# Attention on one core: the vector engine's order within a unit, and softmax sums by a reduction

## The reference, cut to what matters

```
q = ln(fp8_linear(x, wq))       # per head of 128, 16 heads
k = ln(fp8_linear(x, wk))       # 8 key heads; cross: from the context
v = fp8_linear(x, wv)
p = softmax(q k^T / sqrt(128))  # 64 x 64 for each head and batch element
o = p v
cat  = [o_self, o_cross]
catq = fp8(bf16(clip(cat / smooth, -448, 448)))
x = x + catq wproj * scale
```

## Time and profile before

| | us |
|---|---|
| median of three runs | 1179.42 |
| lowest, highest | 1179.37, 1182.78 |
| the profiled execution | 1184.29 |
| its span, first to last instruction | 1182.6 |
| TensorE busy (matmul) | 897.4 |
| VectorE busy | 909.8 |
| ScalarE busy | 727.6 |
| GpSimd busy | 391.3 |

### The profile page before, as it was taken

How to read it: one execution, slowest core, us unless ns; L and a number is a source line. 1 busy time by engine, 2 the same in 40 slices (tenths; PEclk the granted TensorE clock), 3 DMA queues, 4 the chain that set the end, 5 groups by cost and what they waited for, 6 DMA issues and landing times. The chain is left out here.

```text
span 1182.6 us, 23732 instructions
## 1 busy us (share of the span) xinstructions
PE 897.4 (76%) x6878; PEld 793.9 (67%) x6878; DVE 909.8 (77%) x2442; ACT 727.6 (62%) x2471; POOL 391.3 (33%) x498
## 2 busy tenths in 40 slices
PE   3720066423999999999998469999999999997638
PEld 2610033213888888888888458888888888887627
DVE  7989989887888888888888447777777777776471
ACT  3454044374878878877887357777777777774313
POOL 0009900000334444444443443343333433333124
PEclk9865589756999999999999569999999999998559
DMA  6022100002000000000000120000000000000400
GB/s 217 1 108 71 36 1 0 0 0 107 2 2 0 0 0 0 0 0 0 0 0 1 46 79 6 6 6 9 4 4 4 9 4 4 0 0 1 147 19 18
DMA packets 18265, 26.95 MB, mean 23 GB/s; under 512 B 1264, under 2 KB 15408, under 8 KB 17456
## 3 DMA queue, kind: packets, MB, share of 16 engines
q1 hardware_dynamic: 17840, 25.41, 6.3%
q0 software_dynamic: 384, 1.05, 0.3%
HBM read 23.83 MB, written 2.62 MB: 22 GB/s over the span
## 5 line engine op out<-in xcount | busy, mean ns | idle before, releaser
L1213 POOL TENSOR_TENSOR c_cat<-c_tb,c_mb 128x512 fp32r<-128x512 bf16 x64 | 74.3, 1161 | 143.8 <-DVE c_tb L1291 143.8
L1213 POOL TENSOR_TENSOR s_cat<-s_tb,s_mb 128x512 fp32r<-128x512 bf16 x64 | 74.1, 1158 | 112.8 <-DVE s_tb L1291 112.8
L1386 ACT ACTIVATE c_p<-c_kT_sc_ps,c_nmax 128x64 f32<-128x64 f32 x256 | 76.7, 312 | 53.5 <-DVE c_nmax L1257 53.5
L1403 PE MATMUL s_qo_ps<-wq,s_xqf 128*128 128x512 f32 x256 | 76.0, 419 | 32.5 <-POOL s_xqf L1195 32.5
L1386 ACT ACTIVATE s_p<-s_kT_sc_ps,s_nmax 128x64 f32<-128x64 f32 x256 | 76.7, 312 | 26.8 <-DVE s_nmax L1257 23.8
L1403 PE MATMUL c_qo_ps<-wq,c_xqf 128*128 128x512 f32 x256 | 77.0, 423 | 17.2 <-DVE wv L645 17.1
L1461 PE MATMUL s_pj_ps<-wp,s_cat 128*128 128x256 f32 x512 | 79.6, 300 | 1.5 <-POOL s_cat L1213 1.5
L1461 PE MATMUL c_pj_ps<-wp,c_cat 128*128 128x256 f32 x512 | 79.0, 298 | 1.5 <-POOL c_cat L1213 1.5
L1218 POOL TENSOR_TENSOR c_pn<-c_p,c_rsum 128x256 f32<-128x256 f32 x64 | 39.2, 613 | 115.0 <-DVE c_rsum L1340 115.0
L1218 POOL TENSOR_TENSOR s_pn<-s_p,s_rsum 128x256 f32<-128x256 f32 x64 | 39.2, 613 | 112.0 <-DVE s_rsum L1340 112.0
L1333 DVE TENSOR_TENSOR c_yb<-c_qo_ps,c_ism 128x512 bf16<-128x512 f32 x64 | 44.3, 692 | 37.8 <-PE c_qo_ps L1438 37.8
(11 more groups left out here) (359 smaller groups left out, 2899.4 us busy)
## 6 DMA issues: line engine op xcount, KB each, us to landing
x_res<-in_x SPq DMA_DIRECT2D x4, 512.0 KB, 6.0
vT<-in_ctxT SPq DMA_DIRECT2D x2, 1024.0 KB, 10.8
tf_work<-in_wqT SPq DMA_DIRECT2D x2, 1024.0 KB, 5.9
tf_work<-in_wprojT SPq DMA_DIRECT2D x2, 1024.0 KB, 5.5
w_work<-in_wqxT SPq DMA_DIRECT2D x2, 1024.0 KB, 6.5
w_work<-in_wkvxT SPq DMA_DIRECT2D x2, 1024.0 KB, 8.2
c_ctx<-in_ctxT SPq DMA_DIRECT2D x16, 128.0 KB, 2.2
w_work<-in_wprojT SPq DMA_DIRECT2D x2, 1024.0 KB, 7.3
```

The costliest lines, as they stand in the source:

```text
L1213: nc.gpsimd.tensor_tensor(cat[out8.o % 2][:], tb[:], mb[:], ALU.subtract).then_inc(cat_ready, 1)
L1386: nc.scalar.activation(pe_s[:, a * S:(a + 1) * S], sc_ps[:, a * S:(a + 1) * S], ACT.Exp, bias=nmax[:, a:a + 1], accum_out=psum_s[:, a:a + ...
L1403: last = nc.tensor.matmul(out_ap, x_col(h), w_pair[part][:, h, c0:c1], start=(n == 0), stop=(n == 2 * KC - 1))
```

## The change

On VectorE's step: all four rounding steps now come first, one after the other, right behind the scaling; then the residual addition (and statistics); then the three Newton steps, and `qn` right behind them; then the maxima; then `kn`. `qn` waits only for the transposes of the query of the unit before, `kn` for those of the key. The exponentials on ScalarE have no accumulator any more; a reduction on VectorE sums the four blocks of `p` (128x256 to 128x4) in front of the reciprocal, which waits for it by a new semaphore.

```diff
@@ VectorE, in step @@
-                    def normalised():
+                    def normalised_query():
                         dve.wait_ge(r_ready, u.count(1, 1))
-                        wait_unit(dve, t_done, u.before(1))
+                        wait_unit(dve, tq_done, u.before(1))
                         nc.vector.tensor_tensor(qn[:].rearrange("p (h d) -> p h d", d=D),
...
+
+                    def normalised_key():
                         dve.wait_ge(v_ready, u.count(1, 1))
+                        wait_unit(dve, t_done, u.before(1))
                         nc.vector.tensor_tensor(kn[:].rearrange("p (h d) -> p h d", d=D),
...
                     if u.live:
                         norm_guess()
-                    for part in range(3):
-                        if f8.live:
+                    if f8.live:
+                        for part in range(4):
                             round8(part)
-                        if u.live:
-                            newton(part)
                     if pj.live and pj.o % UT == UT - 1:
...
-                    if f8.live:
-                        round8(3)
+                    if u.live:
+                        for part in range(3):
+                            newton(part)
+                        normalised_query()
                     if sm.live:
                         maxima()
                     if u.live:
-                        normalised()
+                        normalised_key()
...
                     if sm.live:
                         dve.wait_ge(exp_ready, sm.count(4, 4))
                         wait_unit(dve, pn_ready, sm.before(1))
+                        nc.vector.tensor_reduce(psum_s[:], pe_s[:].rearrange("p (a t) -> p a t", a=4), AX.X, ALU.add
+                                                ).then_inc(sum_ready, 1)
+                        dve.wait_ge(sum_ready, sm.count(1, 1))
                         nc.vector.reciprocal(rsum[:], psum_s[:]).then_inc(rsum_ready, 1)
@@ ScalarE, in step @@
                             nc.scalar.activation(pe_s[:, a * S:(a + 1) * S], sc_ps[:, a * S:(a + 1) * S], ACT.Exp,
-                                                 bias=nmax[:, a:a + 1], accum_out=psum_s[:, a:a + 1]
-                                                 ).then_inc(exp_ready, 1)
+                                                 bias=nmax[:, a:a + 1]).then_inc(exp_ready, 1)
```

More of the change, by code:

```diff
@@ L1143, in attention_stage @@
         sc_done, max_ready, exp_ready = sg("sc_done"), sg("max_ready"), sg("exp_ready")
+        sum_ready = sg("sum_ready")
         rsum_ready, pn_ready = sg("rsum_ready"), sg("pn_ready")
```

## The result

The changed kernel takes 1311.9 us (median of four runs, 1308.1 to 1313.7) against 1180.3 us; the ratio is 1.111, 95% interval 1.107 to 1.114. The profiled execution has a span of 1311.6 us, 129 us over the 1182.6 us of the trace that the earlier trace rows come from. The forecast was +111 us, 1290.4 us, with a range up to 1320.

The account below looks back on a forecast made before the run. The vector engine's loop was taken to bind, by 0.2 us over TensorE. First stage 67 us plus second stage 46 us, less 2 us, gave +111 us, 1290.4 us, with a range of 1263 to 1320.

Parts of the forecast that it names:

- The hold by `cat`: VectorE's second Newton step is held until GpSimd's `cat` ends: 0.91 us in each of 61 units a stage.
- The bound with a second step free under `cat`: Second Newton step not held, third held instead: `qn` 1.72 us after `tb`, 0.20 us less a unit, 24 us in all.
- The sum: New VectorE reduction of the exponentials in front of the reciprocal: 0.40 us, and 0.04 for the wait behind it.
- `yb` to the sum of squares 0.69: VectorE loop term: 0.69 us between these starts, with the reciprocal.
- the 1.04 us to the clip: VectorE loop term: 1.04 us from the start of the sum of squares to the clip.
- The units that carry more: Units with casts, GpSimd additions, residual addition or statistics pay extra: means 6.88 and 6.81 us against the ordinary 6.58.
- rival 3: TensorE, less busy, is at times granted its lower clock, 1.2 GHz: 71 us more, 1361 us; chance 0.06.
- The upper end: 1320 us, if `cat` is prolonged by 0.08 us (10 us) and the exponentials come late (20 us).
- Exponentials at nothing: ScalarE, outside the loop, saves the accumulator reads: gains nothing, but lets exponentials end at +2.00 us, before the sum at +2.11.
- The upper bound for slow ones, 20 us: Exponentials on ScalarE still 0.30 us apart would end at +2.27 us, costing the loop 0.16 us, 20 us in all.
- Rival 1: `cat` doesn't hold the Newton steps: +15 us in the first stage, +3 in the second, 1197 us; chance 0.09.
- The rival "faster": Sum costs nearly nothing, Newton runs free, TensorE's 5.43 us a unit decides: at most 33 us gained, 1146 us; chance 0.03.

Follow-up runs that it names:

- the kernel without it: Changed kernel with one more wait on GpSimd, so the subtraction into `cat` starts only after the unit's third Newton step: 1207.5 us.
- other orders: Kernels with accumulators, no sum, residual addition and statistics behind `kn`, and `tb` and maxima behind `qn` in either order: 1168.1 and 1168.7 us against the kernel before's 1180.1 to 1180.7.

## Why the prediction was right, and what it undersized

- **The hold by `cat`.** No row of the kernel before had this pair; it was carried over from other pairs, and it is shown now by the trace and by two experiments that change the start or the length of `cat`. `tb` to `qn` was put at 1.92, with the second step held, and at 2.12 behind the residual addition; it is so in 65 and 30 units. In 24 units, those with the index 0 and 1 of a round, the second step slips in front of `cat` and the third is held instead, with `qn` at +1.80; the forecast did not have that. The margin is small: the second step starts 0.54 us after `tb` (put at 0.61), `cat` 0.50, but 0.59 in these 24. The hold is worth about 104 us: the kernel without it is at 1207.5. The bound with a second step free under `cat` is out: whenever it starts there it is held. Nor did `cat` get longer (1.16 us).
- **The Trainium skill's rule** ("SBUF — State Buffer", section "SBUF: two separate sides"), an exclusive lock for the whole instruction: with `cat` at 1.16 us the step takes 1.15, with 0.43 it takes 0.42. The trace agrees in all 122 cases. Not everything on VectorE is held, though: in the kernel before, 61 `qn` a stage start under `cat` and keep their 0.68 us; in the changed kernel the statistics (at 872.30 in the trace, under a `cat` from 871.83 on), which read SBUF, keep their 0.43 us in all 15 cases. In the changed kernel itself no maxima and no `kn` lie beside GpSimd work, so there they say nothing.
- **The sum** was put at 0.40 plus 0.04 and takes 0.41 plus 0.03. But the reduction's cost in the loop was undersized: the sum of squares also starts 0.08 us later behind the reciprocal, which the term "`yb` to the sum of squares 0.69" left out, and takes 0.95 us instead of 0.92, which the 1.04 us to the clip left out: 0.11 us a unit. And the turn of the loop, 0.39 us in one unit of eight, was in no term. Together 0.11 + 0.05 = 0.16 us.
- **The units that carry more** were a little oversized: the second rounding step ends 0.08 us late, not 0.13 (0.37 instead of 0.29), since it starts 1.39 after the sum of squares and GpSimd's addition ends at 1.61, and the scaling with the cast is held 0.50, not 0.60. That gives back some 0.06 us in the first stage. In the second, units with casts take 0.58 us more than ordinary ones (7.28 against 6.70), where 0.73 was forecast: 0.04 us in the mean.
- **The sum of all.** Steady intervals are 6.99 and 6.93 us, forecast 6.88 and 6.81: 0.11 and 0.12 too little, 61 times each, 14 us of the 18 that the spans differ from the forecast. Of the rest, some 2 us lie in the first intervals of the two stages and 2 us outside of them.
- **The clock (rival 3).** In the first stage the granted clock is 0.97 in the mean from 300 to 720 us, where it was 1.00 (300 to 650 us): with TensorE busy 339 of 420 us it falls to the lower of its two levels, 1.2 GHz, eight times for a short while. So rival 3 came true in a small part: five intervals of the steady first stage are 0.2 to 0.5 us longer than those at the same place in other rounds, about 1.5 us together. In the second stage it stays at 1.00 (780 to 1200 us), with TensorE busy 359 of 420 us.
- **The range.** That 1311.9 us lies inside it is partly luck. The upper end stood on a longer `cat` and on late exponentials, and neither came; what lifted the time by 22 us over the forecast were terms that the sum didn't have.
- **Exponentials at nothing.** Right in size: without the accumulator reads four of them take 0.93 us, and the vector engine doesn't wait in front of the sum. The upper bound for slow ones, 20 us, stood on the sum alone; the order without the sum showed that the square of k, queued behind them, is the nearer reader.
- **Rival 1** (1197 us) describes what the order costs without the hold; measured 1207.5. Its intervals are 6.05 and 6.20 us where the rival said 6.02 and 6.10, and the terms above account for part of that. The rival "faster" lives only in other orders: 1168 us.

## What to carry to other kernels

Between GpSimd and VectorE the place of a short instruction counts for more than its length: look in the trace for small SBUF operations on VectorE that last as long as a neighbour on GpSimd, and put beside a GpSimd operation work that isn't held: here what reads PSUM, and the statistics. When an operation on GpSimd starts decides which vector instructions are held, so a wait added on GpSimd can make the kernel faster. And idle time in front of a group of instructions isn't free to fill: nothing may wait for what moves, and what the idle time had covered (here holds by casts) comes back at up to its full price.

## What was not expected of the hardware

Where the last instruction of a round stands behind a wait that is met late, the turn of the instruction loop leaves VectorE idle for 0.38 us in the changed kernel, in all twelve turns of steady rounds; with a 0.41 us instruction behind that one it is 0.15 us, and the kernel before shows none. The reduction over 768 elements takes 0.95 us instead of 0.92, and `qn` 0.69 instead of 0.68, in the changed kernel; why is open. A GpSimd subtraction of 128 columns takes 0.43 us, one of 512 takes 1.16, so by an estimate from these two (a straight line through them) 0.19 us of it doesn't depend on the columns.
